# Router to experts in a 4096-token, one-core kernel: the first tile's product order, the VectorE list, the loads and two buffers' homes

## The reference, cut to what matters

```python
logits = (h @ router_w.T + router_b).reshape(T, O, E)        # O = 512, E = 8
probs = softmax(logits, axis=-1)
w, sel = top_k(probs, 2);  w = w / w.sum(-1, keepdims=True)
c = zeros((T, E)).at[t_idx, sel].add(w)                        # weights summed over all 512 columns
expert_out = einsum('th,eoh->teo', h, expert_w) + expert_b
x = x + einsum('te,teo->to', c, expert_out)
```

## Time and profile before

| what | value |
|---|---|
| time, median of 3 (lowest to highest) | 2383.99 us (2379.42 to 2384.05) |
| time of the profiled execution | 2383.81 us |
| its span | 2382.0 us |
| TensorE busy | 2314.8 us, 97% |
| VectorE busy | 1676.1 us, 70% |
| ScalarE busy | 1143.8 us, 48% |
| DMA moved | 184.61 MB, mean 78 GB/s |

### The profile page before, as it was taken

One profiled execution on the slowest core, in us unless ns is written; L12 is line 12 of the kernel. 1 busy time (PEld: TensorE's weight loads), 2 busy tenths in 40 slices (PEclk: granted clock), 3 DMA queues, 4 the chain that ended last, 5 costly groups with the idle time before them and its releaser, 6 DMA issues.

```text
span 2382.0 us, 30406 instructions
## 1 busy us (share of the span) xinstructions
PE 2314.8 (97%) x10280; PEld 1902.9 (80%) x10288; DVE 1676.1 (70%) x2497; ACT 1143.8 (48%) x1678; POOL 8.9 (0%) x16
## 2 busy tenths in 40 slices
PE   6999999999999999999999999999799999999999
PEld 4767788888888887888888888887688888888887
DVE  6885434343434434788888888999998888888884
ACT  5653323232332324788888888887432222222221
POOL 0000000000000000000000000000000000000000
PEclk9999999999999999999999999999999999999999
DMA  5313211111202113221111111123522222222220
GB/s 173 106 62 95 95 36 55 35 55 35 70 21 73 56 62 151 97 76 62 62 62 57 62 59 64 53 74 125 194 93 93 78 76 92 91 76 79 92 79 22
DMA packets 106589, 184.61 MB, mean 78 GB/s; under 512 B 12466, under 2 KB 45746, under 8 KB 105266
## 3 DMA queue, kind: packets, MB, share of 16 engines
q1 hardware_dynamic: 54946, 124.84, 15.1%
q10 hardware_dynamic: 51600, 59.25, 7.5%
HBM read 122.72 MB, written 61.34 MB: 77 GB/s over the span
## 4 chain that ended last, share of the span: by engine, by line
PE 87%; issue 6%; DVE 5%; ACT 2%; DMA 1%; ACTq 0%; SPq 0%; POOLq 0%; POOL 0%; DVEq 0%
PE slot L1393 15%; PE plane L1524 10%; PE plane L1526 10%; PE plane L1528 10%; PE ex L1566 9%; PE ex L1570 9%; PE ex L1568 9%; PE pj L1406 7%; PE slot L1446 3%; PE slot L1368 1%; PE slot L1435 1%; DVE q_scale L964 1%; PE slot L1425 1%; ACTq L707 0%; DVE q_res L984 0%
## 5 line engine op out<-in xcount | busy, mean ns | idle before, releaser
L1393 PE MATMUL slot<-y_hi,wgu 128*128 128x512 f32 x1024 | 405.4, 396 | 11.7 <-DVE q_scale L964 11.6
L1566 PE MATMUL ex<-ew_hi,hb 128*128 128x512 f32 x1024 | 400.9, 391 | 16.4 <-DVE ew_lo L1280 11.2
L1524 PE MATMUL plane<-rw_hi,hb 128*128 128x512 f32 x1024 | 399.6, 390 | 1.6 <-ACT plane L796 0.9
L1393 PE MATMUL slot<-y_lo,wgu 128*128 128x512 f32 x1024 | 401.0, 392 | 0.0
L1570 PE MATMUL ex<-ew_lo,hb 128*128 128x512 f32 x1024 | 400.3, 391 | 0.0
L1568 PE MATMUL ex<-ew_hi,hb 128*128 128x512 f32 x1024 | 400.2, 391 | 0.0
L1526 PE MATMUL plane<-rw_hi,hb 128*128 128x512 f32 x1024 | 399.2, 390 | 0.0
L1528 PE MATMUL plane<-rw_lo,hb 128*128 128x512 f32 x1024 | 399.1, 390 | 0.0
L904 ACT ACTIVATE ex<-eb_sb 128x512 f32<-128x512 f32 x248 | 149.4, 602 | 461.0 <-DVE acc L1319 396.0
L1252 DVE SCALAR_TENSOR_TENSOR lead_in<-code_in,wts 128x1024 bf16<-128x1024 bf16 x256 | 311.9, 1218 | 1.8 <-DVE code_in L1197 0.4
L1566 PEld LDWEIGHTS ex<-ew_hi,hb 128*128 128x128 f32 x1024 | 193.4, 189 | 58.3 <-issue 7.8
(11 more groups left out here) (120 smaller groups left out, 3101.0 us busy)
## 6 DMA issues: line engine op xcount, KB each, us to landing
hb<-h_scratch SPq DMA_DIRECT2D x34, 512.0 KB, 3.3
h_scratch<-ht ACTq DMA_DIRECT2D x64, 256.0 KB, 3.1
code_scratch<-half_code SPq DMA_DIRECT2D x64, 256.0 KB, 2.0
half_in<-code_scratch SPq DMA_DIRECT2D x32, 512.0 KB, 3.4
hb<-h_scratch ACTq DMA_DIRECT2D x30, 512.0 KB, 3.6
q_raw<-in_w_ffn SPq DMA_DIRECT2D x21, 512.0 KB, 3.9
x_scratch<-x_res ACTq DMA_DIRECT2D x8, 1024.0 KB, 4.4
rraw<-in_rwT SPq DMA_DIRECT2D x8, 1024.0 KB, 11.1
```

Of the source, the lines that this page charges most:

```text
L1393: last = mm(slot[s % 2][:, g, :], wgu[:, c, r * P:(r + 1) * P], y[:, c, :], start=(c == 0 and v == 0), stop=(c == DC - 1 and v == 1))
L1524: mm(plane[b][:, :, :], hb[:, u, c, 0, :], rw_hi[:, w, c, o], start=False, stop=False, skip_group_check=True)
L1566: mm(ex[e][:, :], hb[:, u, c, 0, :], ew_hi[:, e, c, :], start=(first and c == 0), stop=False, skip_group_check=True)
```

## The change

Six edits:

1. Expert weights are laid out in device memory so that each partition's row of one expert is one contiguous piece of 8 KB (`ewT` as E, P, DC*D) in place of four pieces of 2 KB.
2. SyncE issues the eight `eraw` loads without the stores of router tile 30 between them; the expert biases are loaded next (they wait only for `seeded`), then the stores, `lead_in` and `half_in`, and the rows of x after the last router half (`lead_ready`).
3. `eb_sb` takes the memory of `bias_sb`, the router's biases, in place of that of `L`. `acc`, `xin` and `res` take that of `top4`, `low4`, `top2`, `m1`, `m2`.
4. TensorE's first tile (`first_experts`) runs the 64 products with high weights of all eight experts first, waiting for `ehi` only, and then the 32 with low weights, waiting for `elo`.
5. VectorE: the last `half` without its join, then the five remaining `ew_lo` splits, the eight expert sums of tile 0, the two joins, the eight bias sums (now last, into `res`), `decode(2)` and the eight `total(2, e)`, and then tile 1.
6. ScalarE: the splits come ahead of the last two `stand`; the first pair of tiles is written out of its loop, and `weigh(2)` stands behind the seeds of tile 0. `store(0)` also waits for the bias sums.

```diff
+        p4 = ExitStack()
+        eb_sb = sb("eb_sb", [P, E, D], F32, p4)
+        p4.close()
         bias_sb = sb("bias_sb", [P, 2, E, HO], F32, p2)
...
         c_ring = sb("c_ring", [P, 4, E], F32, p2)
+        L = sb("L", [P, 2, E, HO], F32, p2)
         p3 = ExitStack()
-        eb_sb = sb("eb_sb", [P, E, D], F32, p3)
         acc = sb("acc", [P, 2, D], F32, p3)
...
         p3.close()
-        L = sb("L", [P, 2, E, HO], F32, p2)
         top4 = sb("top4", [P, 4, HO], F32, p2)
...
         X1T = x1_dram.rearrange("(n p) d -> n p d", p=P)
-        EWT = ewT.rearrange("(c p) (e o) -> e p c o", p=P, o=D)
...
                 for e in (2 * b, 2 * b + 1):
-                    sp.dma_start(eraw[:, e, :, :], EWT[e]).then_inc(eraw_in[e], 16)
-                if b == 0:
-                    spill(NT - 2, 0, 2 * NT - 3, 2 * NT - 2, 2 * NT - 2)
+                    sp.dma_start(eraw[:, e, :, :].rearrange("p c o -> p (c o)"), ewT[e]).then_inc(eraw_in[e], 16)
             load_h(1, 1)
-            sp.wait_ge(joined, 2 * NT)
-            sp.dma_start(xin[:, 0, :], X1T[0]).then_inc(x1_in[0], 16)
+            sp.wait_ge(seeded, NT * PT)
             sp.dma_start(eb_sb[:, :, :], eb).then_inc(eb_in, 16)
-            sp.dma_start(xin[:, 1, :], X1T[1]).then_inc(x1_in[1], 16)
+            spill(NT - 2, 0, 2 * NT - 3, 2 * NT - 2, 2 * NT - 2)
             load_lead(2, 0)
...
             load_halves(2)
+            sp.wait_ge(lead_ready, 2 * NT)
+            sp.dma_start(xin[:, 0, :], X1T[0]).then_inc(x1_in[0], 16)
+            sp.dma_start(xin[:, 1, :], X1T[1]).then_inc(x1_in[1], 16)
             spill(NT - 1, 1, 2 * NT - 1, 2 * NT, 2 * NT)
...
-                if isinstance(n, int) and n == 0:
-                    sp.wait_ge(bias_step, 1)
-                else:
-                    sp.wait_ge(exp_step, wait)
+                sp.wait_ge(exp_step, wait)
                 sp.dma_start(xin[:, u, :], one(X1T, n + 2)).then_inc(x1_in[u], 16)
...
             evacuate(NT - 1, 1, (3,))
-            split_expert(2)
+            for e in range(2, E):
+                split_expert(e)
             stand(NT - 1, 0)
-            split_expert(3)
-            split_expert(4)
             stand(NT - 1, 1)
-            for e in range(5, E):
-                split_expert(e)
             def store(n, u):
+                if isinstance(n, int) and n == 0:
+                    act.wait_ge(bias_step, E)
                 act.wait_ge(exp_step, n * E + E)
...
             act.wait_ge(eb_in, 16)
-            with act.Fori(0, NT // 2 - 1) as m:
+            def pair(m):
                 for u in range(2):
-                    weigh(m * 2 + (u + 2), u, m + 1)
+                    if not (isinstance(m, int) and u == 0):
+                        weigh(m * 2 + (u + 2), u, m + 1)
                     for e in range(E):
                         seed_expert(m * 2 + u, e)
+                    if isinstance(m, int) and u == 0:
+                        weigh(2, 0, 1)
                     store(m * 2 + u, u)
...
+            pair(0)
+            with act.Fori(1, NT // 2 - 1) as m:
+                pair(m)
             for e in range(E):
...
                 split_expert(e)
-            half(NT - 1, 1, 1, NT // 2 - 1)
-            split_expert(3)
-            split_expert(4)
-            join(NT - 1, 1)
-            for e in range(5, E):
+            half(NT - 1, 1, 1, NT // 2 - 1, joins=False)
+            for e in range(3, E):
                 split_expert(e)
-            def bias(n, e, k, trip):
+            def bias(e):
+                if e:
+                    dve.wait_ge(bias_step, e)
+                nc.vector.scalar_tensor_tensor((res if e == E - 1 else acc)[:, 0, :], eb_sb[:, e, :], c_ring[:, 0, e:e + 1],
+                                               acc[:, 0, :], ALU.mult, ALU.add).then_inc(bias_step, 1)
+            def expert(n, e, k, trip):
                 u = k % 2
-                if e == 0:
-                    dve.wait_ge(x1_in[u], trip * 16)
-                    dve.wait_ge(summed, n * E + E)
-                else:
-                    dve.wait_ge(bias_step, n * E + e)
-                nc.vector.scalar_tensor_tensor(acc[:, u, :], eb_sb[:, e, :], c_ring[:, k, e:e + 1],
-                                               (xin if e == 0 else acc)[:, u, :], ALU.mult, ALU.add).then_inc(bias_step, 1)
-            def expert(n, e, k, trip):
-                u = k % 2
-                base = acc
+                first = isinstance(n, int) and n == 0
                 if e != 0:
                     dve.wait_ge(exp_step, n * E + e)
-                elif isinstance(n, int) and n == 0:
-                    dve.wait_ge(bias_step, E)
                 else:
...
                     dve.wait_ge(summed, n * E + E)
-                    base = xin
                 dve.wait_ge(ex_filled, n * E + (e + 1))
...
                     dve.wait_ge(out_done[u], trip * 16)
-                nc.vector.scalar_tensor_tensor((res if e == E - 1 else acc)[:, u, :], ex[e][:, :], c_ring[:, k, e:e + 1],
-                                               base[:, u, :], ALU.mult, ALU.add).then_inc(exp_step, 1)
+                nc.vector.scalar_tensor_tensor((res if e == E - 1 and not first else acc)[:, u, :], ex[e][:, :],
+                                               c_ring[:, k, e:e + 1], (xin if e == 0 else acc)[:, u, :],
+                                               ALU.mult, ALU.add).then_inc(exp_step, 1)
...
+            for e in range(E):
+                expert(0, e, 0, 0)
+            for s in range(2):
+                join(NT - 1, s)
             dve.wait_ge(eb_in, 16)
+            dve.wait_ge(exp_step, E)
             for e in range(E):
-                bias(0, e, 0, 1)
-            for n in range(4):
+                bias(e)
+            decode(2, 2)
+            for e in range(E):
+                total(2, e, 2)
+            for n in range(1, 4):
                 tile(n, n, n // 2)
...
-            def experts(m, u, first=False):
+            def experts(m, u):
...
                 for e in range(E):
-                    if first:
-                        if e >= 4:
-                            pe.wait_ge(evac, NT * PT - 3 + e - 4)
-                        pe.wait_ge(elo, e + 1)
-                    else:
-                        pe.wait_ge(ex_seeded, m * (2 * E) + (u * E - E + e + 1))
+                    pe.wait_ge(ex_seeded, m * (2 * E) + (u * E - E + e + 1))
                     for c in range(DC):
-                        mm(ex[e][:, :], hb[:, u, c, 0, :], ew_hi[:, e, c, :], start=(first and c == 0), stop=False,
-                           skip_group_check=True)
-                        mm(ex[e][:, :], hb[:, u, c, 1, :], ew_hi[:, e, c, :], start=False, stop=False,
-                           skip_group_check=True)
+                        mm(ex[e][:, :], hb[:, u, c, 0, :], ew_hi[:, e, c, :], start=False, stop=False, skip_group_check=True)
+                        mm(ex[e][:, :], hb[:, u, c, 1, :], ew_hi[:, e, c, :], start=False, stop=False, skip_group_check=True)
                         last = mm(ex[e][:, :], hb[:, u, c, 0, :], ew_lo[:, e, c, :], start=False, stop=(c == DC - 1),
...
-            experts(0, 0, first=True)
+            def first_experts():
+                pe.wait_ge(hb_in[0], NT // 2 * 16 + 16)
+                for e in range(E):
+                    if e >= 4:
+                        pe.wait_ge(evac, NT * PT - 3 + e - 4)
+                    pe.wait_ge(ehi, e + 1)
+                    for c in range(DC):
+                        for v in range(2):
+                            mm(ex[e][:, :], hb[:, 0, c, v, :], ew_hi[:, e, c, :], start=(c == 0 and v == 0), stop=False)
+                for e in range(E):
+                    pe.wait_ge(elo, e + 1)
+                    for c in range(DC):
+                        last = mm(ex[e][:, :], hb[:, 0, c, 0, :], ew_lo[:, e, c, :], start=False, stop=(c == DC - 1))
+                    last.then_inc(ex_filled, 1)
+            first_experts()
             experts(0, 1)
...
         "rb": np.broadcast_to(g["L1_ffn_router_b"].reshape(1, 2, D // 2, E).transpose(0, 1, 3, 2), (P, 2, E, D // 2)),
-        "ewT": g["L1_ffn_expert_w"].transpose(2, 0, 1).reshape(D, E * D),
+        "ewT": g["L1_ffn_expert_w"].reshape(E, D, DC, P).transpose(0, 3, 2, 1).reshape(E, P, DC * D),
         "eb": np.broadcast_to(g["L1_ffn_expert_b"].reshape(1, E, D), (P, E, D)),
```

## The result

The changed kernel takes 2372.15 us (median of five, 2371.66 to 2377.29). The kernel before takes 2379.42 (median of five, 2378.41 to 2384.05). The ratio is 0.9966 with a 95% interval of 0.9955 to 0.9978: faster by 0.34%. I had forecast 2377.7 within 2373 to 2382.

The account below looks back on a forecast made before the run. VectorE's list was taken to bound the seam between router and experts, TensorE's matmul count everything behind it. From 2383.8 us, minus 6.9 gained at tile 2, plus 0.8 for the clock, came 2377.7 us, range 2373 to 2382.

Parts of the forecast that it names:

- VectorE's list: Seam between router and experts: VectorE's steps summed forward from 1661.33 put expert 1 of tile 1 at 1720.0 us.
- rival E: VectorE's sums and totals in a row cost no more than spread out (0.67 and 1.15 us); time 2375.8; chance 0.04.
- High products: TensorE's first tile: 64 products needing only `ew_hi`, paced by loads and ScalarE, ending at about 1677.6 us.
- waits at tile 2: TensorE waits for VectorE's sums through ScalarE's seeds until 1716.2, then 1721.5 us, against 1728.40 before: gain 6.9 us.
- D: TensorE's first tile: `ew_hi` late, high products get no head start; forecast's time again; chance within the forecast's 0.60.
- B: TensorE is not held at tile 2, VectorE's list being shorter or the second seed not binding; 2370.6 us; chance 0.07.
- The rows of x: `xin`, behind 12.85 MB of loads, lands at 1686.4 us, wanted by VectorE at 1687.8: no cost, 1.4 us of cover.
- A: Rows of x late: whole queue at 356 GB/s, landing at 1690.0, 2.2 us late; time 2379.9; chance 0.18.
- C: Slower than before: load queue collapses, VectorE's first expert sum waits; 2389.7 us at 280 GB/s; chance 0.05.
- The clock's term: TensorE's slow clock after waits at tile 2: costs between 0 and 1.7 us, taken as 0.8.
- the spread of single runs: Whole-kernel times: 4.6 us between lowest and highest shown, counted as some 2 us to each side of the forecast.
- VectorE's three waits: VectorE's old list: idle of 1.28 us, 0.42 us and the join's wait; the change saves 2.7 us of waits.

Follow-up runs that it names:

- e6: Changed kernel with VectorE summing each expert of tile 1 first, bias sums and totals behind, and two `hb` loads ahead of stores: 2370.17 and 2370.54 us.
- e7: Changed kernel with both the old order of TensorE's products and the old order of VectorE's sums: 2376.05 us, ratio 0.9978 to the kernel before.
- e3: Changed kernel with TensorE's first tile in the old order, an expert's 12 products behind its low weights: 2378.7 us.
- e4: Changed kernel with VectorE's sums of tile 0 in the old order, bias sums first and totals between expert sums: 2378.75 us.

## Why the prediction was wrong in time and right in mechanism

- **VectorE's list** (the forward sum). Forecast 1687.8, 1694.0, 1695.2, 1701.4, 1704.8, 1714.8, 1720.0; the trace has 1688.10, 1694.26, 1695.46, 1701.64, 1705.07, 1715.09, 1720.32. Each step is right to 0.1 us, all shifted by the 0.27 with which VectorE starts (1661.60 for 1661.33). Totals in a row stand 1.27 apart, dependent sums 0.79, so rival E falls. The rule of the Trainium skill ("VectorE: DVE Perf Modes", the section on the DRAIN you cannot avoid), that the semaphore between chained operations costs nothing extra, does not show in this trace either: a sum starts 0.79 us behind the sum that it waits for, and other work starts 0.66 behind a sum.
- **TensorE.** High products to about 1678.3 (forecast 1677.6), tile 1 without a wait, waits at tile 2 until 1716.52 and 1721.75 (1716.2 and 1721.5). D's condition, high products 10 us late, did not arise. B falls, and e6 shows that it was the order of VectorE's list that ruled it out.
- **The rows of x.** No wait. They landed at 1687.2 to 1687.4 where I had 1686.4, with about half the cover that I had counted (0.7 to 0.9 us for 1.4). The sum had left out that SyncE issues them only at 1677.19. Loads of weights came 2.48 us apart (ScalarE's splits start at that pace), 427 GB/s over 1655 to 1665 and 431 over 1665 to 1675, more than the 415 taken. A and C fall, A by a margin under 1 us. The 358 GB/s of the Trainium skill ("DMA: Bandwidth & Descriptors", Specifications) is exceeded here for 20 us; that row gives it as half of what two cores share, and here one core runs.
- **The clock's term** was mis-sized: I took 0.8 of bounds 0 and 1.73. The slow stretch fell on tile 2's expert 0, which had slack; the twelve matmuls from 1721.75 to 1724.62 took 2.87 in place of 2.72, so the term was 0.15. With 0.27 for the late start, the sum for this trace is 6.9 - 0.15 - 0.27 = 6.5, and 6.5 is what the two profiled executions differ by.
- **The step that failed is the last one: "the spread of single runs (4.6 us between the lowest and highest shown)", of which I counted "some 2 us to each side by the runs".** I had treated 2379.42, 2384.05 and 2383.99 as one cloud around 2384. They are two levels, 5.0 us apart, set ahead of the seam, and the forecast of 2377.7 is one for the upper level (2377.03 measured there, a median of three). The median of the result fell on the lower level, where the forecast's own gain of 6.1 from 2378.75 gives 2372.6, outside the range by itself. On which level a median of five falls is chance as far as any run shows; had it been the upper one, the range would have held by luck as much as by reading. The forecast's gain of 6.1 us against 6.6 and 6.7 by level would have stood at either level; its time could only stand at one.
- **What the change is made of.** By level 6.6 to 6.7 us in all: loads, homes and the place of the last half 3.0 to 3.2 of it, nearly all of that VectorE's three waits; layout by itself nothing; the rest products and sums together. No run takes loads, homes and the last half apart. Either order alone takes 1.1 to 1.5 off the 3.4 to 3.7 that are left (e7 against e3 and e4), the second one the other 2.1 to 2.3. For the order of products alone (e4) that first part is all clock: VectorE's list is as long as in e7, and only the low clock falls elsewhere.

## What to carry to other kernels

Where one engine's explicit list sets the start of another, add up the list forward with start-to-start spacings from the trace, dependent and independent ones apart; here it came out right to 0.1 us over 59 us. Then order the list by who is waited for: the same operations with expert sums put first were worth another 6 us. And before forecasting a time, look whether the runs of the kernel before form one group or two, forecast the difference from a trace, and say for which level the time is meant. Where a program has such levels, compare the time from one mark to another inside the traces: that leaves out what happens ahead of the edit.
